# One order for another: the calls of all five engine programs of a transformer block laid anew

## The reference

```python
mod = (silu(c) @ wmod).reshape(8, 6, 1, 256)          # sa, ca, ga, sb, cb, gb; |ga|, |gb| >= 0.25
h = layernorm(x) * (1 + ca) + sa
a = layer_norm(h, ln1)                                # attention: 16 heads of 16, window of 128 back
s = q @ k.T * 0.25 + band;  ctx = softmax(s) @ v
y = h + ctx @ Wo + bo
y = y + gelu(layer_norm(y, ln2) @ W1 + b1) @ W2 + b2
x = x + ga * y
h = layernorm(x) * (1 + cb) + sb
prev = shift(h, one token)
xr, xk = mu_r*h + (1-mu_r)*prev, mu_k*h + (1-mu_k)*prev
x = x + gb * sigmoid(xr @ Wr) * (relu(xk @ Wk)**2 @ Wv)
```

## Time and profile before

| | |
|---|---|
| median of 3 runs | 688.05 us (682.75 to 689.03) |
| the profiled execution | 686.02 us |
| its span, first to last instruction | 684.3 us |
| mean granted TensorE clock | 0.974 of full speed |
| busy: TensorE, VectorE, ScalarE, GpSimd | 86%, 74%, 74%, 54% |

### The profile page before, as it was taken

The page is one execution under the profiler, slowest core; times in us unless marked ns, Lnnn a source line. Parts: engine busy times, 40 slices in busy tenths (PEclk is TensorE's granted clock), DMA queues, the critical chain, the costliest instruction groups (busy, mean ns, idle before and its releaser), DMA issues.

```text
span 684.3 us, 18053 instructions
## 1 busy us (share of the span) xinstructions
PE 589.2 (86%) x6814; PEld 470.4 (69%) x6814; DVE 509.6 (74%) x1058; ACT 508.7 (74%) x780; POOL 366.8 (54%) x514
## 2 busy tenths in 40 slices
PE   5686697998789898899889898989898988899986
PEld 2555586877577676767676767677777766777775
DVE  5576577777788788788888888888987687564563
ACT  2623755579698979897989888998898886894642
POOL 5202444481639554865677475937593657564231
PEclk9878999999999999999999999999999999999999
DMA  3734212232023032403232223222311332101010
GB/s 129 276 72 102 64 43 48 62 100 67 19 67 98 18 89 55 117 24 86 65 79 72 73 66 82 80 60 64 76 57 46 73 72 64 32 2 48 31 39 32
DMA packets 56867, 47.05 MB, mean 69 GB/s; under 512 B 26235, under 2 KB 48061, under 8 KB 56782
## 3 DMA queue, kind: packets, MB, share of 16 engines
q1 hardware_dynamic: 53798, 43.85, 23.9%
q10 hardware_dynamic: 2984, 2.05, 1.2%
HBM read 18.11 MB, written 4.23 MB: 33 GB/s over the span
## 4 chain that ended last, share of the span: by engine, by line
PE 39%; ACT 29%; issue 10%; DVE 9%; SPq 7%; DMA 3%; POOL 2%; ACTq 0%; DVEq 0%; POOLq 0%
ACT bank L942 6%; ACT p L874 5%; SPq L2163 4%; PE bank L230 4%; SPq L2165 4%; ACT hid_hi L952 3%; PE bank L425 3%; PE bank L463 3%; PE bank L451 3%; PE bank L426 3%; PE bank L427 3%; ACT L942 3%; PE quad L325 3%; ACT kt_hi L846 2%; DVE nmax L1359 2%
## 5 line engine op out<-in xcount | busy, mean ns | idle before, releaser
L1927 POOL TENSOR_SCALAR_AFFINE_SELECT p<-p 128x448 f32<-128x448 f32 x64 | 40.4, 632 | 218.7 <-ACT p L874 179.1
L874 ACT ACTIVATE p<-quad,scale_s 128x768 f32<-128x768 f32 (+1 forms) x102 | 81.9, 821 | 39.6 <-PE quad L325 28.5
L889 ACT ACTIVATE p_hi<-p 128x1344 f16<-128x1344 f32 x64 | 83.9, 1322 | 14.3 <-POOL p L1932 7.1
L1940 POOL TENSOR_TENSOR p_lo<-p,p_hi 128x1344 f16<-128x1344 f32 x32 | 87.6, 2736 | 5.0 <-ACT p_hi L889 5.0
L325 PE MATMUL quad<-q_st,k_st 100*128 100x192 f16 (+3 forms) x576 | 61.4, 229 | 22.4 <-ACT p L874 7.6
L1359 DVE TENSOR_REDUCE nmax<-quad 128x8 f32<-128x1032 f32 x64 | 78.9, 1234 | 2.2
L408 PE MATMUL bank<-bt_hi,w_hi 128*128 128x256 f16 x256 | 70.5, 275 | 9.5 <-DVE hid_lo L1432 8.3
L1432 DVE SCALAR_TENSOR_TENSOR hid_lo<-bank,inv_f,hid_hi 128x512 f16<-128x512 f32 x64 | 48.0, 749 | 37.8 <-ACT hid_hi L952 37.6
L425 PE MATMUL bank<-w_hi,hid_hi 128*128 128x256 f16 x256 | 70.0, 274 | 0.9 <-DVE hid_lo L1432 0.8
L409 PE MATMUL bank<-bt_lo,w_hi 128*128 128x256 f16 x256 | 70.2, 274 | 0.0
L410 PE MATMUL bank<-bt_hi,w_lo 128*128 128x256 f16 x256 | 70.2, 274 | 0.0
(11 more groups left out here) (226 smaller groups left out, 1636.7 us busy)
## 6 DMA issues: line engine op xcount, KB each, us to landing
k_st<-kt_hi SPq DMA_DIRECT2D x120, 64.0 KB, 2.0
v_blk<-vn SPq DMA_DIRECT2D x64, 66.0 KB, 2.2
x<-x SPq DMA_DIRECT2D x16, 256.0 KB, 2.8
out<-x SPq DMA_DIRECT2D x16, 256.0 KB, 2.1
q_st<-qt_hi SPq DMA_DIRECT2D x120, 32.0 KB, 1.9
k_st<-kt_lo SPq DMA_DIRECT2D x60, 64.0 KB, 2.0
...
```

The lines of the kernel that those rows point to most:

```text
L874: e.activation(p32[gp % 2][:, c0:c0 + 2 * w].rearrange("p (n c) -> p n c", n=2), quad[:, b0:b0 + 2, 0:w], ACT.Exp, scale=scale_s[:, 1:2]). ...
L889: e.activation(p_hi[gp % 2][:, :].rearrange("p (n c) -> p n c", c=GW)[:, :, 0:QW], p32[gp % 2][:, :].rearrange("p (n c) -> p n c", c=QW), ...
L1940: e.tensor_tensor(cut(p_lo), p32[gp % 2][:, :].rearrange("p (n c) -> p n c", c=QW), cut(p_hi), ALU.subtract).then_inc(s_plp, 1)
```

## The change

No call is added or taken away and no body changes but for one wait of GpSimd at the end of its `setup_const`. The lists of calls of PE, ACT, DVE, POOL and SP are written anew; the loop now covers fewer turns, and more of the start and of the last batches is written out. The core of the diff:

```diff
@@ PE, start
             setup_first()
+            setup_attn()
             setup_mod()
-            setup_attn()
             setup_peak()
+            setup_row()
+            warm(0, 9)
             transposes_a(0)
-            warm(0, 9)
...
@@ ACT, the first gelus
+            exps(11, 0, 2)
+            gelu(0, 0, 2)
+            high_f(0, 0, 1)
+            max_copy(3)
             exps(11, 2, 4)
             high_p(10)
...
             exps(12, 0, 2)
             exps(12, 2, 4)
-            gelu(0, 0, 2)
-            high_f(0, 0, 1)
+            high_p(11)
             gelu(0, 2, 4)
-            high_f(0, 1, 2)
-            high_p(12)
             exps(13, 0, 2)
             exps(13, 2, 4)
+            split_v(2, 0)
+            high_f(0, 1, 2)
+            gelu(0, 4, 6)
...
@@ DVE, the loop
-            for b in range(2, B):
-                u, gp = 2 * b, 8 * b
...
+            for b in range(1, 5):
+                u = 2 * b
+                gp = 8 * b
+                maxima(u + 3, 3)
+                low_m(u + 3)
+                low_b(u)
+                residual_b(u - 1)
+                low_qk(u + 4)
+                gated(u - 2)
+                normalise(gp + 9)
+                maxima(u + 4, 0)
+                output(u - 2)
...
+                residual_b(u)
+                scale_x(b + 3)
+                low_qk(u + 5)
+                gated(u - 1)
...
@@ SP, start
             load_mod()
+            load_w2()
             load_attn()
-            rows_mod()
             load_rest()
             load_x(1)
+            rows_mod()
+            stacks(0, 0, 2)
             load_mod_a(1)
-            load_w2()
-            stacks(0, 0, 2)
             stacks(1, 0, 2)
...
@@ SP, the loop
-            for b in range(2, B):
-                u, gp = 2 * b, 8 * b
-                load_mod_g(b - 3)
-                load_mod_o(b - 4)
-                store(u - 8)
-                load_residual(u - 6)
-                stacks(u - 2, 0, 4)
-                load_v(b - 1, 0)
-                stacks(u - 1, 0, 4)
-                load_v(b - 1, 1)
-                u, gp = 2 * b + 1, 8 * b + 4
-                store(u - 8)
-                load_x(b + 1)
-                load_residual(u - 6)
-                load_mod_a(b + 1)
...
+            for b in range(3, 6):
+                u = 2 * b
+                stacks(u, 0, 4)
+                load_residual(u - 4)
+                load_v(b, 0)
+                stacks(u + 1, 0, 4)
+                store(u - 5)
+                load_mod_o(b - 2)
+                load_x(b + 2)
+                load_v(b, 1)
+                load_residual(u - 3)
+                load_mod_g(b - 1)
+                store(u - 4)
+                load_mod_a(b + 2)
```

1253 lines of the change are left out of this document (819 added, 434 removed).

## The result

The change is slower: 709.74 us median (707.88 to 713.88, four runs) against 687.99 (682.75 to 689.03, four runs), a ratio of 1.034 with a 95% interval of 1.0271 to 1.0409. The same order measured again beside the experiments (the run after_again) took 714.73 against 686.83, ratio 1.0394 (1.0339 to 1.0449). The profiled execution took 707.88 us, its span is 706.1, and the mean granted clock 0.955 of full speed (0.974 before).

What follows compares the result with a forecast made beforehand. No engine alone was taken as the bound: TensorE, ScalarE and VectorE are 84 to 89% busy and wait for each other. Terms summed to -6.4 us from 686.02, 679.6, plus 0.4 for the runs' mean: 680.0 us, range 668 to 694.

Steps and rivals of the forecast that it cites:

- SyncE in the even half: Loop: stack DMAs ahead of the residual load and output earlier remove ScalarE's wait for k_st; -5.0 us over four batches.
- VectorE in the odd half: Loop: low_qk behind residual_b and scale_x delays the scores; 0 to 2.2 us a batch, taken as 0.5, +2.0 over four.
- Splits: Loop: fewer split pairs, so one ScalarE activation does what two did; 0.4 us a batch, -1.6 if all on the path.
- Start to projection 6: Four terms: to projection 2 +1.0, projections 2 to 3 +1.5, 3 to 4 -1.8, 4 to 6 -0.5 us.
- the 14 warms taken away between projections 3 and 4: Start: TensorE, the bound there, loses 14 warms, 4.4 us; between -4.4 and +1, taken as -1.8 us.
- The end: From 504.5 us on: last maxima and scores closer together, one more pair of table loads; between +3 and -6, taken -2.0.
- Signs: No k_st waits; halves 10 to 11 near 36, next near 34.5; 36 loads; projection 4 at 145 to 147, 6 near 218.
- B: Loop: the next wait replaces the one removed, TensorE and ScalarE meeting again; about 0 gain, 686 to 688 us; chance 0.20.
- C: Projections 3 to 6: ScalarE becomes the bound, table loads delay exps; 693.7 us, 695 to 696 against the median; chance 0.11.
- D: Before projection 2: a lower granted clock, about 5 us; 691 us, or 693 with the loop's gain lost; chance 0.05.

Runs made afterwards that it cites:

- the cuts: The change's order up to head 7 (695.91 us) or up to head 14 (702.36 us), then the order of before.
- sp_first: Kernel before, SyncE alone: in even halves 6 to 12 the stack DMAs go ahead of the store and residual load; 681.60 us against 686.02.
- odd_before: The change with odd halves 7, 9, 11 and 13 in the order of before on all five engines; 711.89 us, ratio 1.0387.
- odd_before2: odd_before with VectorE's scale_x moved back into the even half ahead of rest_v and residual_b behind gated; 699.46 us, ratio 1.021.
- end_first: The change with all five engines in the order of before from head 15 to group 60, then its own order; 713.67 us, last stretch 152.7.

## Why the prediction was wrong, by its own steps

The three parts side by side, forecast by the sum's terms and measured by the cuts: start +0.2 and +9.1, loop -4.6 and +6.5, end -2.0 and +12.4. All three failed, the end by most.

**SyncE in the even half, -5.0: right.** sp_first gave -4.4 by itself, the wait for `k_st` went, and the even halves became shorter as the mechanism says. By its one profile only 2.7 us of that lie from head 6 to 15.

**VectorE in the odd half, +2.0: the step that failed first.** The bound of 2.2 a batch counted `scale_x` alone, by its own duration, and nothing in the sum priced the rest of the odd half's new order. The row that came to stand between `low_m` and `low_qk` is `residual_b`, statistics and `scale_x`, 3.8 us (328.34 to 332.17). Taking it away between odd_before and odd_before2 gave 12.4 us, 3.1 a batch: outside the bound. In the change's own order neither of the two places that I tried for the row gave any gain, since waits for `cx` or `tr`, `hid_lo` and `p` stand right behind it. So what failed is the step that gave the row a price of its own: the odd half's order as a whole, from after_again to odd_before2, is worth 10.1 us from head 6 to 15 (14.0 against the first profile). VectorE's 497 instructions between heads 6 and 14 also took 248.2 us in the first profile and 247.5 in after_again for 242.6 in before; what that adds is open.

**Splits, -1.6: there, but not in the time.** From head 6 to 14 ScalarE is busy for 245.1 us in the first profile and 244.6 in after_again, for 247.5 in before. That is 2.3 to 2.8 us less work, and the stretch was longer all the same; by how much it would have been longer without this no run shows.

**Start to projection 6, +0.2 by four terms: wrong.** The first profile agreed (220.3), the median of 15 says 227.7, +8. Up to head 3 it is about +2 (forecast +2.5). From 3 to 6 the change takes 109 to 111 us for 104.4 in before and 102.6 in sp_first (forecast -2.3). Set beside before, after_again has +0.6 between heads 3 and 4 and +5.0 from there to 6. Each of these lies within the bounds that I gave it, near or at the upper end; the values that I took inside the bounds were too low. Its head 5 comes early only because both downs of the first half still stand behind it; before had done them, and the next stretch, 42.5 us for 37.0, pays. I had read the 14 warms taken away between projections 3 and 4 as a gain of TensorE, but its idle time there rose from 1.3 us to 3.4, and between heads 4 and 5 it was 7.0 us in after_again. Why these stretches have so much idle time is open, and so is the part of the table loads in it.

**The end, -2.0: wrong by some 14, the largest miss.** I had bounded it by +3; the stretch behind head 15 alone lost 11.9. I had read TensorE's idle time of 19.4 us before as room for the changed order, and had not followed the handovers from the last row maxima to the first gelu: between head 15 and 600 us TensorE has no wait above 1.48 us in before, and in the change one of 4.03 and three of 1.67 to 2.55. The first part of the loss is where `mix(10)`, `low_m(15)` and `exps(59)` stand behind each other on three engines; none of the moves tried there helped, and which one step makes it is open. The second came to light in end_first: the empty wait for the maxima's DMA. From 153.7 us the order of before in the first part alone leads to 152.7, the filled wait to 146.2, and the remaining 4.0 to 142.2 weren't traced further.

**Signs and rivals.** Of the signs named, the wait on `k_st` went and there are 36 loads of 1.28 us. Heads 10 to 11 and 11 to 12 are 37.0 and 37.9 us in place of about 36 and 34.5, head 4 came at 143.5 in the first profile and at 148.5 in after_again, and the stretch from 3 to 4 took 32.0 in both. B came nearest: another wait took the place of the one removed, but at a loss, not at zero. C: the loads can't be priced by their count, since the kernel with four fewer was slower; and a load is still 1.28 us and no more, as in after_again, where the activation before ends at 155.67:

```profile
155.69 1.28 ACT L1255 ACT_TABLE_LOAD   x1
156.98 0.99 ACT L1255 ACTIVATE bank<-bank,bias,scale_g 128x256 f32<-128x256 f32 x2
```

By the Trainium skill (ScalarE: Activation LUTs, What ACT_TABLE_LOAD costs) a drain of about 1.38 us would come on top of the load; the trace has 0.02 us ahead of it and 0.01 behind it. D, the clock, I had looked for in one place of the start only and given 0.05. It was lower in all three stretches. In the loop and at the end it fell where the order had made longer waits (0.91 in two odd halves, 0.56 behind the 3.70 us in end_first) and added to them; how much of the start's loss is its doing is open. What I lacked was a case in which several of these go wrong at once: no rival that I had priced from rows reached past 696.
